# Cross-attention stack on one Trainium2 core: layer four's score transposes leave the four-bank tile for single banks

## The reference, cut to what matters

```python
def attention(q, k, v, mask):                       # 16 heads of 16
    scores = jnp.einsum('bhqd,bhkd->bhqk', q, k) / jnp.sqrt(jnp.float32(HD))
    scores = scores * mask - 10000.0 * (1.0 - mask)
    probs = jax.nn.softmax(scores, axis=-1)
    return jnp.einsum('bhqk,bhkd->bhqd', probs, v)
...
q, k, v = split(layernorm(x, ln1) @ w_qkv + b_qkv)  # self attention, one mask for all
x = x + attention(q, k, v, ltor_mask) @ w_ao + b_ao
q = layernorm(x, ln2) @ w_q + b_q                   # cross attention, a mask per sequence
k, v = split(ctx @ w_kv + b_kv)
x = x + attention(q, k, v, cross_mask) @ w_co + b_co
x = x + gelu(layernorm(x, ln3) @ w1 + b1) @ w2 + b2
```

## Time and profile before

| | us |
|---|---|
| median of 3 runs | 2174.29 |
| lowest and highest | 2172.28, 2174.91 |
| the profiled execution's own time | 2172.8 |
| its span, first to last instruction | 2171.1 |
| TensorE busy | 1946.4 (90%) |
| VectorE busy | 1069.7 (49%) |
| ScalarE busy | 956.5 (44%) |
| GpSimd busy | 707.0 (33%) |
| layer four's attention in the span | 1717 to about 2055 |

### The profile page before, as it was taken

How to read it: one execution, slowest core, us unless ns; L and a number is a source line. 1 busy time by engine, 2 the same in 40 slices (tenths; PEclk the granted TensorE clock), 3 DMA queues, 4 the chain that set the end, 5 groups by cost and what they waited for, 6 DMA issues and landing times.

```text
span 2171.1 us, 39280 instructions
## 1 busy us (share of the span) xinstructions
PE 1946.4 (90%) x16109; PEld 1652.6 (76%) x16109; DVE 1069.7 (49%) x1946; ACT 956.5 (44%) x2550; POOL 707.0 (33%) x819
## 2 busy tenths in 40 slices
PE   6788887898999999999999999999979778878698
PEld 5566665787888888888888888888867656756587
DVE  4444544544444444444454444445443577676743
ACT  4244333333444444443434444444434467666633
POOL 3222222402331413233233141323321267666500
PEclk9799998999999999999999999999999899999999
DMA  3000001100010100000001010000020000000000
GB/s 106 10 7 2 7 2 40 56 1 20 10 30 1 39 1 11 20 1 20 11 11 49 1 40 1 12 20 1 20 86 1 10 2 2 7 1 6 2 18 22
DMA packets 28035, 38.45 MB, mean 18 GB/s; under 512 B 1344, under 2 KB 19408, under 8 KB 27856
## 3 DMA queue, kind: packets, MB, share of 16 engines
q1 hardware_dynamic: 27856, 35.95, 5.3%
HBM read 33.84 MB, written 2.10 MB: 17 GB/s over the span
## 4 chain that ended last, share of the span: by engine, by line
PE 77%; DVE 10%; ACT 7%; issue 3%; POOL 2%; DMA 0%; ACTq 0%; SPq 0%; DVEq 0%; POOLq 0%
PE ps_high L195 40%; PE ps_four L195 7%; PE ps_four L2574 5%; PE ps_four L2594 5%; PE ps_four L2583 2%; PE ps_four L2378 2%; PE ps_high L2470 2%; PE ps_high L2361 1%; ACT l_pt L1709 1%; PE ps_four L2386 1%; PE ps_high L2399 1%; POOL l_sm L1563 1%; DVE l_sm L2126 1%; PE ps_four L2500 1%; PE ps_four L2510 1%
## 5 line engine op out<-in xcount | busy, mean ns | idle before, releaser
L1805 ACT ACTIVATE l_prob<-ps_four,l_mx 128x129 f32<-128x129 f32 x512 | 181.7, 368 | 571.9 <-DVE l_mx L2161 571.9
L1597 POOL TENSOR_TENSOR l_prob<-l_prob,l_mx 128x516 f32<-128x516 f32 x128 | 134.3, 1050 | 732.9 <-DVE l_mx L2168 732.9
L195 PE MATMUL ps_high<-ctxT,l_wk 128*128 128x512 f32 x768 | 214.8, 416 | 0.0
L195 PE MATMUL ps_high<-l_hT,l_wq 128*128 128x512 f32 x768 | 209.8, 408 | 0.0
L195 PEld LDWEIGHTS ps_high<-l_wo,l_ao 128*128 128x128 f32 x1536 | 196.2, 189 | 13.4 <-DVE l_ao L2180 3.1
L195 PE MATMUL ps_high<-l_wv,ctxT 128*128 128x512 f32 x768 | 203.6, 401 | 1.7 <-ACT l_qT L1786 1.4
L195 PE MATMUL ps_high<-l_wo,l_ao 128*128 128x256 f32 x1536 | 202.0, 281 | 1.7 <-DVE l_ao L2180 1.7
L1563 POOL TENSOR_TENSOR l_sm<-l_sm,l_mask 128x1024 f32<-128x1024 f32 x64 | 150.3, 2372 | 120.4 <-DVE l_sm L2126 120.4
L195 PEld LDWEIGHTS ps_high<-l_wv,ctxT 128*128 128x128 f32 x768 | 144.7, 192 | 44.2 <-ACT l_qT L1786 9.9
L195 PEld LDWEIGHTS ps_high<-ctxT,l_wk 128*128 128x128 f32 x768 | 138.8, 194 | 23.4
L2180 DVE SCALAR_TENSOR_TENSOR l_ao<-ps_four,columns,l_ao 128x512 fp32r<-128x512 f32 x128 | 96.1, 751 | 117.0 <-ACT l_ao L1815 117.0
(11 more groups left out here) (286 smaller groups left out, 3870.4 us busy)
## 6 DMA issues: line engine op xcount, KB each, us to landing
l_staging<-in_L_xattn_wv SPq DMA_DIRECT2D x8, 512.0 KB, 4.5
l_staging<-in_L_xattn_wk SPq DMA_DIRECT2D x8, 512.0 KB, 3.8
l_staging<-in_L_xattn_wq SPq DMA_DIRECT2D x8, 512.0 KB, 4.3
l_staging<-in_L_xattn_wo SPq DMA_DIRECT2D x8, 512.0 KB, 3.5
ctx_tok<-in_ctx SPq DMA_DIRECT2D x8, 256.0 KB, 3.0
x_tok<-in_x SPq DMA_DIRECT2D x4, 512.0 KB, 5.3
l_raw_w<-in_L_xattn_mlp_w SPq DMA_DIRECT2D x2, 1024.0 KB, 7.5
l_staging<-in_L_xattn_w_fc SPq DMA_DIRECT2D x4, 512.0 KB, 4.9
```

Source lines behind the costliest of these rows:

```text
L195: ins = e.matmul(out, a, b, start=start and i == 0, stop=stop and i == 2, skip_group_check=not check)
L1597: e.tensor_tensor(pr[:, :, 0:S + 1], pr[:, :, 0:S + 1], mx[:, 3, :].unsqueeze(2).to_broadcast([P, GB, S + 1]), ALU.mult).then_inc(sem("poo ...
L1805: ins = e.activation(pr.t[:, b, 0:S + 1], banks[b // 2].t[:, (b % 2) * (S + 2):(b % 2) * (S + 2) + S + 1], ACT.Exp, bias=mx[:, 1, b:b + 1] ...
```

## The change

The transposes of `l3_probs` no longer use the four-bank tile. Each group of four goes to a single bank of the ring `over` (banks 4 to 7), with a full and an empty count of its own. The stage is emitted in two halves (groups 0 and 1; groups 2 and 3) with a `fill()` between them; the `fill()` that stood between `probs` and `shifted` is the one now between the halves, so a step still has four. The scores keep the four-bank tile to themselves. In `values`, both products are emitted first and the two copies after, each with a `yield` ahead of it, and one more at the end; the banks are held until then. In `output`, `x_add` comes two yields later, and the two banks are held until it. `L3_RATE` goes from 2.1 to 2.3. The exponentials stay one per bank, the number of instructions that compute is the same on each engine.

```diff
-L3_RATE, L3_SLACK = 2.1, 2
+L3_RATE, L3_SLACK = 2.3, 2
...
         for i in range(2):
             self.pl.emit("x_add", key, i, g=g, src=(kind, src), events=events)
-            if kind == "side":
-                self.pl.free("side", src, i)
+            if kind == "side" or key[0][:2] == "l3":
+                self.pl.free(kind, src, i)
...
                 pl.bank(self.side, "out32", t, h)
                 pl.emit("out32", t, h, w=W[w], over=("pool.l3_ao", n))
-                pl.free("out32", t, h)
                 yield
             pl.free("ao", t, by=("full", "out32", t, 1))
+            yield
+            yield
             self.x_done[g] = self.x_add(t, g, t, self.x_done[g], kind="out32")
...
                 if kind == "a":
-                    pl.emit("l3_values", g, h, hs=("hs", u), hs_done=begun[t]["hs_done"], dst=("vv", t))
+                    pl.emit("l3_values", g, h, hs=("hs", u), hs_done=begun[t]["hs_done"])
                 else:
-                    pl.emit("rows2", ("l3v", *t), h, w="l3_w_kv", off=D, src=("ctx", g), src_done=None, dst_key=("vv", t))
+                    pl.emit("rows2", ("l3v", *t), h, w="l3_w_kv", off=D, src=("ctx", g), src_done=None, dst_key=None)
+                yield
+            for h in range(2):
+                yield
+                pl.emit("l3_vv", t, h)
                 pl.free("rows", ("l3v", *t), h)
-                yield
             if kind == "a":
                 pl.free("hs", u, by=("full", "rows", ("l3v", *t), 1))
             ready[t] = ("empty", "rows", ("l3v", *t), 1)
+            yield
...
-        def probs(n):
-            pl.slot(pt, "pt", n)
-            pl.bank(four, "four", "l3", n, 1)
-            pl.emit("l3_probs", n)
-            pl.free("four", "l3", n, 1)
-            pl.free("sm", n, by=("full", "four", "l3", n, 1))
+        def probs(n, half):
+            if half == 0:
+                pl.slot(pt, "pt", n)
+            for r in (2 * half, 2 * half + 1):
+                pl.bank(over, "probT", n, r)
+                pl.emit("l3_probs", n, r)
+                pl.free("probT", n, r)
+            if half == 1:
+                pl.free("sm", n, by=("full", "probT", n, 3))
...
             if 1 <= n <= N:
-                probs(n - 1)
+                probs(n - 1, 0)
             fill()
+            if 1 <= n <= N:
+                probs(n - 1, 1)
             if n < N:
                 shifted(n)
             fill()
...
-        def l3_probs(n):
-            bk, pt = use["four", "l3", n, 1], use["pt", n]
+        def l3_probs(n, r):
+            bk, pt = use["probT", n, r], use["pt", n]
             q.wait_ge(*pl.event(pt.before))
             table(ACT.Exp)
-            for r in range(4):
-                if r < 3:
-                    q.wait_ge(sem("pe.l3_probs"), 3 * n + r + 1)
-                else:
-                    q.wait_ge(*pl.event(("full", "four", "l3", n, 1)))
-                ins = e.activation(pt.t[:, r, :], bk.t[:, r, :], ACT.Exp, scale=float(DH) ** -0.5)
-            ins.then_inc(bk.slot.empty, 1)
+            q.wait_ge(*pl.event(("full", "probT", n, r)))
+            e.activation(pt.t[:, r, :], bk.t, ACT.Exp, scale=float(DH) ** -0.5).then_inc(bk.slot.empty, 1)
...
+        def l3_vv(t, h):
+            two_parities(use["rows", ("l3v", *t), h], use["vv", t], h, ("full", "rows", ("l3v", *t), h))
...
-        def l3_probs(n):
+        def l3_probs(n, r):
             sm = use["sm", n].t
-            bk = fill("four", "l3", n, 1)
-            for r in range(4):
-                q.wait_ge(*pl.done("dve.l3_shift:s" if r < 2 else "act.l3_shift", n))
-                for x in range(4):
-                    ins = e.transpose(bk.t[:, r, x * S:(x + 1) * S], sm[:, 4 * r + x, :], self.ident[:])
-                ins.then_inc(sem("pe.l3_probs") if r < 3 else bk.slot.full, 1)
+            q.wait_ge(*pl.done("dve.l3_shift:s" if r < 2 else "act.l3_shift", n))
+            bk = fill("probT", n, r)
+            for x in range(4):
+                ins = e.transpose(bk.t[:, x * S:(x + 1) * S], sm[:, 4 * r + x, :], self.ident[:])
+            ins.then_inc(bk.slot.full, 1)
...
-            q.wait_ge(*pl.event(("empty", "four", "l3", n, 1)))
+            q.wait_ge(*pl.event(("empty", "probT", n, 3)))
```

More of the change, by code:

```diff
@@ L1258, in plan_l3 @@
         attention.close()
-        probs_done, over_done = ("full", "four", "l3", N - 1, 1), ("full", "over", "l3", N - 1)
+        probs_done, over_done = ("full", "probT", N - 1, 3), ("full", "over", "l3", N - 1)
         self.mlp_tiles("l3e", scope, (probs_done, probs_done, over_done, ("pool.l3_scores", N - 1)))
@@ L1873, in rows2 @@
         def rows2(p, h):
+            if p[0] == "l3v":
+                return
             two_parities(use["rows", p, h], use[pl.info["rows2", p, h]["dst_key"]], h, ("full", "rows", p, h))
@@ L2139, in l3_shift @@
             e.tensor_reduce(mx.t[:, 8:16], sm[:, 8:16, :], AX.X, ALU.max, negate=True).then_inc(sem("dve.l3_shift:b"), 1)
-        def l3_values(g, h):
-            f, bk = pl.info["l3_values", g, h], use["rows", ("l3v", "a", g), h]
-            two_parities(bk, use[f["dst"]], h, ("full", "rows", ("l3v", "a", g), h))
+        def l3_vv(t, h):
+            two_parities(use["rows", ("l3v", *t), h], use["vv", t], h, ("full", "rows", ("l3v", *t), h))
         def l2_v(tgt, b):
@@ L2212, in vector_program @@
                       mlp_w=mlp_w, mhs=mhs, hid3=hid3, norm_xn=norm_xn, norm_split=norm_split, x_add=x_add, rows=rows,
-                      l3_const=l3_const, l3_scores=l3_scores, l3_shift=l3_shift, l3_values=l3_values,
+                      l3_const=l3_const, l3_scores=l3_scores, l3_shift=l3_shift, l3_vv=l3_vv,
                       l2_v=l2_v, l2_scores=l2_scores, l2_norm=l2_norm, l2_tr=l2_tr,
```

## The result

| | before | after |
|---|---|---|
| median of the runs measured side by side, us | 2173.28 (2169.05 to 2174.91, 4 runs) | 2185.18 (2182.75 to 2186.57, 4 runs) |
| ratio to before, 95% interval | 1 | 1.0057 [1.0039, 1.0075] |
| the profiled execution's own time, us | 2172.8 | 2182.75 |
| span, us | 2171.1 | 2181.0 |
| first to last masking (31 steps), us | 322.2 | 331.9 |

The changed kernel is 0.57% slower: 37 us above the forecast and outside the range. The span grew by 9.9 us, the 31 steps by 9.6 (2046.18 - 1714.32, against the earlier trace rows); the rest moved by 3 us each way (start 3.2 earlier, tail 3.4 longer), as it does between executions.

A forecast was written before the change was run, and what follows sets the result against it. In layer four's attention no engine is the bound; waits are, 70.8 us above a floor of 8.11 us per step. Terms -18 - 8 - 3 + 3 = -26 us gave 2148 us, range 2122 to 2178.

The forecast's parts named there:

- Side work keeps its place within two yields: Rate 2.3 gives 27 more yields, `values` and `output` ask for 30 more; side work stays in place: 0 us.
- Scores free of the exponentials: TensorE's scores end earlier, lead over masking 3.6 us; 2.3 us gained in each of eight full runs: -18 us (-14 to -26).
- TensorE idles, since it can't work ahead: Reading of the profile: between the eleven steps with more than 8.11 us of TensorE work, TensorE stands idle.
- Copies and additions later: VectorE no longer stands before `x_add` and value copies with row maxima behind: 4.4, 2.4 and 1.6 us, -8 us (0 to -15).
- the 23.6 us: VectorE's waits for products of the side work before the change, 15.3 + 8.3 us; forecast near zero after.
- Waits inside full runs: Of 20 waits of about 1 us before TensorE's scores, three inside full runs count: -3 us (0 to -6).
- Seven uses of four banks: Transposes share banks 4 to 7 with `over` and side work; waits for banks charged at +3 us (0 to +28).
- VectorE's second operation: L2136 beside GpSimd takes 2.12 us; the 8.11 us floor already holds that: 0, by durations alone at most +7 us.
- The stages outside: Parts of the kernel outside layer four's attention stretch: forecast wrong if they move by over 4 us.
- Given back: Rival: gains met by 20 to 30 us of bank waits, or copy waits become score waits; about 2172 us, chance 0.14.
- Clock: Rival: single banks break up TensorE's work so full steps run cold at 1.2 GHz; 2208 us, chance 0.03.
- Banks behind the shift: Rival: TensorE's transposes of groups 2 and 3 and `over` wait for held banks; +29 us, 2203 us, chance 0.14.

The follow-up runs named there:

- after_r21: The changed kernel with `L3_RATE` back at 2.1, nothing else changed; ratio 1.0022 to the kernel before.
- after_late_r24: The changed kernel with GpSimd's bias addition (`x_bias`) three yields later and `L3_RATE` 2.4; ratio 0.9992 to the kernel before.
- delays_pair: The kernel before, four-bank tile still shared, with the later copies and additions, rate 2.3, and ScalarE's two norm halves together; ratio 1.0006 to the kernel before.
- banks_only: The kernel before with the transposes in four single banks, undivided and in their old place, rate 2.1; ratio 1.0009 to the kernel before.
- warm: The kernel before with transposes in single banks, undivided, rate 2.1, plus 20 more transposes of group 1 in ten units; ratio 1.0014 to the kernel before.
- after_pair: The changed kernel with ScalarE's two halves of the norm kept together in layer four's norms; ratio 1.0023 to the kernel before.

## Why the prediction was wrong

The forecast was too low by 37 us. Some 24 to 31 us of that are gains of the sum that did not come, since the two lists without holes measure 0.9992 and 1.0022; 8 to 14 us are the phase of the side work, which the sum put at 0.

**The step that failed on the sign** is "Side work keeps its place within two yields: 0", bounds -1 and +4. The count of yields stands (57). But the order against the scores is what counts, and two norms landed where three engines wait for one another. Cost: 8 us by the rate alone (after_r21, 1.0022), 14 us by rate and a later bias addition (after_late_r24, 0.9992), two to over three times the upper bound. Where the holes stand could have been seen ahead, though not what closing them gives, which the experiments above overrated twice: writing out the new order of stages needs no chip, and a norm's reciprocal root just behind the scores with the bias addition ahead of the next ones is visible in it.

**"Scores free of the exponentials", -18**, was mis-sized: 0 alone (1.0009). The lead was worked out on quiet steps, where TensorE goes from transposes straight to scores, and there it came nearly as said: the scores of 2027.11 end 3.2 us ahead of the masking at 2031.47, against 1.8 us before and 3.6 forecast. (In a quiet step at the lower clock it is 1.7 us, 1946.81 against 1948.51.) In a full step the side work stands between them, and TensorE's order is what it was. "TensorE idles, since it can't work ahead" stood in my own reading; I then gave it the tile and not the order. With the order added, on top of banks and delays, the term measures 0.9992 - 0.9907 = 0.85%, 18 us. That it is the forecast's number is luck: it is the price of another change, and its interval reaches from some 14 to 23 us.

**"Copies and additions later", -8**, measured 0 alone (delays_pair). The step of the earlier trace rows did fall, from 15.47 to 11.19 us in delays_pair, the 4.4 us worked out. But the one before it grew from 11.15 to 13.12, another from 12.01 to 15.66, and steps 11 to 21 together take 118.7 us against 119.7. A step was priced by itself, with the steps around it held still; as I read it, TensorE's work of those steps is the sum that has to pass. "If VectorE does not wait there it waits for scores" was said of part of the 23.6 us and held for nearly all. The 23.6 us also left out copies that wait for another product (L2486, 3.2 us); the waits ahead of additions and copies were 26.8 us before, and 17.8 in the changed kernel.

**"Waits inside full runs", -3**: the waits went, no gain can be seen apart. **"Seven uses of four banks", +3**: right in size. TensorE's waits for banks sum to 10 us, under the 15 named, and one bank fewer cost 0.27% (5.9 us) in the list of banks_only. **"VectorE's second operation", 0**: right. The operation beside GpSimd takes 2.11 us (median of L2143; 2.11 before), and the shortest steps keep the floor, 8.1 us, in every kernel run. Its mean fell from 1897 to 1831 ns instead of rising, since in late steps, where GpSimd has ended, it runs alone (1.22 us); in the two holes it does not (2.15 and 2.12 us). **The stages outside** moved by 3 us each way, within the 4 named. Of the signs listed ahead, the two waits for the tile went as said; the wait for scores (38.1 us, not 15 to 20), the 31 steps (331.9 us, not 296) and the clock (0.88, not 0.92) did not.

**The rivals.** "Given back", 0.14, is what the change does in the better of the two lists without holes: 2172 forecast, 0.9992 measured, and 1.0022 in the other. Its second sentence, waits under "copies" become waits for scores, is the mechanism; its waits for banks were not. "Clock", 0.03: the clock did fall in the stretch, 0.92 to 0.88, where gaps of up to 2.5 us stand ahead of the second half of the transposes; warm, which fills them, has 0.92 again. The Trainium skill, "TensorE: Matmul & The Clock Gate", section "A second HAM failure mode: psum-queue depth-cycling", tells of a kernel whose cycling through banks leaves small idle times, lets the clock swing and lowers the throughput. The trace agrees on the clock (though the gaps here are waits for ScalarE's shift and not for a bank), but not on the time: warm measured 1.0014 against 1.0009. "Banks behind the shift" had the sign and not the cause. No rival held the phase of the side work.

**Left open.** after_pair and after_r21 stay 0.2% above the kernel before and after_late_r24 does not. The waits of `out32` for a bank that a copy holds do not explain it: 3.3 us and 1.6 us in the two, 2.7 us in the third. No run settles it.

## What to carry to other kernels

In a kernel whose engines share one order of work, freeing a buffer gives nothing until the order lets the freed engine run ahead: ask for each wait removed what stands next in that engine's list, and change tile, order and the reader's place together. Print the order of the list before and after any change of rate or yields, and look for a short chain over several engines that has come to stand between two stages of the main loop; the place of two instructions was worth 3 to 7 us here, where the design in its first order gained nothing. And measure a change at two or three rates before judging it.

## What was not expected of the hardware

TensorE's granted clock and the time came apart: from 0.88 back to 0.92 in a stretch of 327 us did not change the time in sum (1.0014 against 1.0009). Some steps got shorter and others longer; perhaps most of the cold instructions follow idle time that covers them (argued, not shown).

GpSimd's instruction on 128x4 elements (L1540) took 2.02 us at 2029.28, nearly as long as a mask addition on 128x1024 (2.34 us each), where its eight calls in the stretch have a median of 1.02 us. The profiled executions of all runs and of the two kernels, 20 in all, hold 160 calls of it: 41 took about 2 us, and each of these starts while VectorE runs its addition on `l_sm` and `l_mx` (L2143 here); of the 119 that took about 1 us none does. The slow ones here end 0.88 us after VectorE's addition (2031.30 against 2030.42), as if it had held them up, and the kernel before has two such calls too. No run changed the overlap by itself.

```profile
2028.32 2.10 DVE L2143 TENSOR_TENSOR l_sm<-l_sm,l_mx 128x1024 f32<-128x1024 f32 x1
2029.28 2.02 POOL L1540 TENSOR_TENSOR l_rs<-l_rs,minus_half 128x4 f32<-128x4 f32 x1
```
